# Norms, additions and slots of the last block: work moved from the vector engine to the scalar engine and GpSimd

## The reference

```python
x = x + _L1_ffn_ref(_layernorm(x), w_gate, w_up, w_down)      # first feed-forward
x = x + _L1_attn_b_ref(_layernorm(x), W_act, W_val, W_rec)    # a scan over time
x = x + _L1_ffn_ref(_layernorm(x), w_gate, w_up, w_down)      # second feed-forward, same weights

# _L1_ffn_ref
h = silu(x @ w_gate) * (x @ w_up)                              # 1024 wide
h_sparse = of every four neighbours of h the two of largest magnitude are kept
return h_sparse @ w_down

# _L1_attn_b_ref
ct = concatenate([x shifted by one position, x])
z = sigmoid(relu(ct @ W_act.T)); re, im = z in pairs
m = cummax(sqrt(re * re + im * im)); re, im = re / m, im / m
kv = associative_scan(complex product, (re, im))
return (kv @ W_val.T) * sigmoid(relu(ct @ W_rec.T)) ** 4
```

## Time and profile before

| what | us |
|---|---|
| median of three runs (1669.57 to 1683.92) | 1672.8 |
| the profiled execution | 1681.59 |
| its span | 1679.8 |
| this block, from its first instruction on DVE to the end | 1209.8 to 1679.8 |
| PE busy in the program (84% of the span) | 1409.5 |
| DVE busy (64%) | 1075.5 |
| ACT busy (37%) | 617.2 |
| POOL busy (17%) | 285.7 |

### The profile page before, as it was taken

The page is one execution under the profiler, slowest core; times in us unless marked ns, Lnnn a source line. Parts: engine busy times, 40 slices in busy tenths (PEclk is TensorE's granted clock), DMA queues, the critical chain, the costliest instruction groups (busy, mean ns, idle before and its releaser), DMA issues. The chain is left out here.

```text
span 1679.8 us, 21713 instructions
## 1 busy us (share of the span) xinstructions
PE 1409.5 (84%) x8144; PEld 1004.7 (60%) x8144; DVE 1075.5 (64%) x2163; ACT 617.2 (37%) x1144; POOL 285.7 (17%) x239
## 2 busy tenths in 40 slices
PE   2799999867999877799966899988579977979698
PEld 2455555456888756688864334433258765766576
DVE  5555454176877456778837566566267688787875
ACT  1254544333333222333321565656522422333221
POOL 1210000034433201233331330200120101011000
PEclk9799897678999988899986999999989998989899
DMA  8715320040000000000024421300000000000000
GB/s 179 97 31 67 53 26 1 1 146 1 1 1 1 1 0 1 1 1 1 1 59 51 86 54 33 48 2 1 1 1 1 1 0 1 1 1 0 13 13 25
DMA packets 23064, 42.01 MB, mean 25 GB/s; under 512 B 4705, under 2 KB 6497, under 8 KB 22833
## 3 DMA queue, kind: packets, MB, share of 16 engines
q1 hardware_dynamic: 22960, 40.64, 13.2%
HBM read 14.54 MB, written 2.10 MB: 10 GB/s over the span
## 5 line engine op out<-in xcount | busy, mean ns | idle before, releaser
L1285 DVE TENSOR_REDUCE attn_negm<-ps 128x2 f32<-128x1024 f32 (+3 forms) x256 | 256.1, 1021 | 124.1 <-PE ps L923 66.3
L1133 ACT ACTIVATE attn_probs<-ps 128x512 f32<-128x512 f32 (+3 forms) x512 | 237.0, 515 | 200.6 <-PE ps L946 124.4
L453 POOL TENSOR_TENSOR moe_h_low<-moe_h,moe_h_high 128x512 fp32r<-128x512 f32 x96 | 137.0, 1429 | 331.7 <-ACT moe_h_high L403 331.7
L937 PE MATMUL ps<-attn_qs,attn_ks 64*128 64x512 f32 (+3 forms) x512 | 156.9, 426 | 37.9 <-ACT attn_probs L1133 35.6
L1645 PE MATMUL ps<-sb_f_down,tail_h 128*128 128x256 f32 x512 | 129.8, 401 | 56.8 <-DVE x L1915 41.1
L1645 PEld LDWEIGHTS ps<-sb_f_down,tail_h 128*128 128x128 f32 x512 | 101.2, 200 | 78.1 <-DVE x L1915 44.1
L913 PE MATMUL ps<-attn_ks,attn_qs 63*128 63x512 f32 (+3 forms) x512 | 122.0, 473 | 29.3 <-DMA attn_ks<-attn_part_low 24.3
L420 ACT ACTIVATE moe_silu<-ps 128x512 f32<-128x512 f32 x96 | 57.4, 598 | 228.6 <-PE ps L326 228.5
L937 PEld LDWEIGHTS ps<-attn_qs,attn_ks 64*128 64x128 f32 x512 | 73.8, 198 | 102.2 <-ACT attn_probs L1133 96.7
L961 PE MATMUL ps<-attn_probs,attn_va 128*32 128x512 f32 (+3 forms) x1024 | 128.9, 580 | 0.0
L913 PEld LDWEIGHTS ps<-attn_ks,attn_qs 63*128 63x128 f32 x512 | 52.8, 202 | 97.8 <-issue 67.0
(11 more groups left out here) (317 smaller groups left out, 3282.8 us busy)
## 6 DMA issues: line engine op xcount, KB each, us to landing
attn_qs<-attn_part_high SPq DMA_DIRECT2D x64, 128.0 KB, 5.1
attn_qs<-attn_part_low SPq DMA_DIRECT2D x32, 128.0 KB, 4.7
attn_ks<-attn_part_high SPq DMA_DIRECT2D x32, 128.0 KB, 6.4
attn_ks<-attn_part_low SPq DMA_DIRECT2D x16, 128.0 KB, 7.1
out_x<-x SPq DMA_DIRECT2D x4, 512.0 KB, 2.6
x<-in_x SPq DMA_DIRECT2D x1, 1536.0 KB, 11.1
attn_qs<-attn_mT SPq DMA_DIRECT2D x64, 4.0 KB
moe_raw<-in_f_gate SPq DMA_DIRECT2D x2, 512.0 KB, 6.9
```

Source lines behind the costliest of these rows:

```text
L453: pool.tensor_tensor(hc.low[:, j % RING, :], h[:, j % RING, :], hc.high[:, j % RING, :], ALU.subtract).then_inc(low_done, 1)
L937: last = pe.matmul(ps[:, SC + k, 0:width2(kt)], ks[e:e + ROWS2, b % 2, key_tile(hd), kt * P:(kt + 1) * P], qs[e:e + ROWS2, b % 2, hd // 2, ...
L1133: act.activation(pr[:, s2 % RING, j, 0:n], ps[:, SC + k, 0:n], ACT.Exp, scale=HD ** -0.5).then_inc(exp_done, 1)
L1285: dve.tensor_reduce(m, ps[:, 2 * half:2 * half + 2, 0:width1(qt)], AX, ALU.max, negate=True).then_inc(r1_free, 1)
```

## The change

The eight norms of the scan's input and of its output leave DVE: ACT copies each row with its sum accumulated, POOL makes the negative mean of it, ACT squares (x - mean) with its sum accumulated, and POOL adds epsilon and raises to the power -0.5 (tensor_tensor with `ALU.pow`; the norms of sequences 1 to 3 at the start take their means and variances from DVE still, and this power from POOL). ACT copies the down sums out of PSUM into `dsum`, on which PE's next pass now waits (`sum_done`), and DVE adds `dsum` to x in one instruction of 128x1024 ahead of the slot's product. The inverse and the scan's output are put ahead of DVE's product too. The array of the scan lies with its segments outermost in a row (`zz`, [P, 2, S1, NS]), so that levels and trees read neighbours in memory; the fill writes into a second array `zt` in order of time, to which ACT copies what the fill doesn't write (`totals`). The running maximum is taken before the root. Jobs stand in other slots. POOL forms the low halves of the weights only after the first norm.

```diff
+    for p in range(PASSES):
+        act_at[added(p) - 1].append(("sum", p))
+        dve_first[added(p)].append(("add", p))
     for b in range(B):
         s = scan_from(b)
-        dve_at[s].append(("stats", "s", b))
+        act_at[s].append(("moments", "s", b))
         pool_at[s].append(("normalise", "s", b))
-        pe_at[s + 2] += [("row", "s", b, c) for c in range(DC)]
-        act_at[s + 2] += [("row", "s", b, c) for c in range(DC)]
-        pe_at[s + 3].append(("act", b, 0))
-        pe_at[s + 4].append(("act", b, 1))
-        act_at[s + 3].append(("act", b, 0))
-        act_at[s + 4] += [("act", b, 1), ("square", b)]
-        dve_at[s + 5].append(("sum", b))
-        act_at[s + 6].append(("root", b))
...
-        dve_at[s + 7] += [("divide", b)] + [("level", b, i) for i in (1, 2, 3)]
-        dve_at[s + 8] += [("level", b, i) for i in (4, 5, 6, 7)]
-        dve_at[s + 9] += [("tree", b, d) for d in TREE[:3]]
-        dve_at[s + 10] += [("tree", b, d) for d in TREE[3:]]
-        dve_at[s + 11].append(("fill", b))
-        pe_at[s + 6].append(("rec", b, 0))
-        act_at[s + 6].append(("rec", b, 0))
-        pe_at[s + 8].append(("rec", b, 1))
-        act_at[s + 8].append(("rec", b, 1))
-        pe_at[s + 12] += [("out", b, m) for m in range(2)]
-        dve_at[s + 12] += [("out", b, m) for m in range(2)]
-        dve_at[s + 13].append(("stats", "f", B + b))
+        pe_at[s + 1] += [("row", "s", b, c) for c in range(DC)]
+        act_at[s + 1] += [("row", "s", b, c) for c in range(DC)]
+        pe_at[s + 2] += [("act", b, 0), ("act", b, 1)]
+        act_at[s + 2] += [("act", b, 0), ("act", b, 1), ("square", b)]
+        dve_at[s + 3] += [("sum", b), ("peak", b)]
+        act_at[s + 3].append(("root", b))
+        dve_first[s + 4].append(("invert", b))
+        dve_at[s + 4] += [("divide", b), ("level", b, 1)]
+        pe_at[s + 5].append(("rec", b, 0))
+        act_at[s + 5].append(("rec", b, 0))
+        dve_at[s + 5].append(("level", b, 2))
+        pe_at[s + 6].append(("rec", b, 1))
+        act_at[s + 6].append(("rec", b, 1))
+        dve_at[s + 6].append(("level", b, 3))
+        dve_at[s + 7] += [("level", b, i) for i in (4, 5, 6)]
+        dve_at[s + 8] += [("level", b, 7)] + [("tree", b, d) for d in TREE[:2]]
+        dve_at[s + 9] += [("tree", b, d) for d in TREE[2:5]]
+        dve_at[s + 10] += [("tree", b, d) for d in TREE[5:]] + [("fill", b)]
+        act_at[s + 10].append(("totals", b))
+        pe_at[s + 11] += [("out", b, m) for m in range(2)]
+        dve_first[s + 13].append(("out", b))
+        act_at[s + 13].append(("moments", "f", B + b))
         pool_at[s + 13].append(("normalise", "f", B + b))
         pe_at[s + 15] += [("row", "f", B + b, c) for c in range(DC)]
         act_at[s + 15] += [("row", "f", B + b, c) for c in range(DC)]
         dve_at[s + 15] += [("row", "f", B + b, c) for c in range(DC)]
 
+    NORMS = [job[1:] for at in act_at for job in at if job[0] == "moments"]
     jobs = Turns([6, 7])
     early = [("row", "f", 0, c) for c in range(DC)]
     for todo in [early, *pe_at]:
...
             def value(b, m):
                 bank = take_bank(("out", b, m))
                 pe.wait_ge(filled, b + 1)
+                pe.wait_ge(totals_done, b + 1)
                 for i in range(2):
...
                 p, j = m // FC, m % FC
                 if j == 0:
-                    at_least(pe, x_done, p)
+                    at_least(pe, sum_done, p)
                 pe.wait_ge(sel_done, m // QUAD + 1)
                 for t in range(NT):
...
+            def root(b):
+                act.wait_ge(peak_ready, b + 1)
+                act.activation(sq[:, 1, :], sq[:, 1, :], ACT.Sqrt).then_inc(root_ready, 1)
+
+            def down_sum(p):
+                act.wait_ge(down_done, FC * (p + 1))
+                at_least(act, x_done, p)
+                act.activation(dsum[:, :, :], ps[:, DOWN:DOWN + 2, :], ACT.Copy).then_inc(sum_done, 1)
+
+            def moments(kind, k):
+                b = k % B
+                n, turn = nb[kind], NORMS.index((kind, k)) + 1
+                at_least(act, squared, turn - 1)
+                if kind == "s":
+                    act.wait_ge(x_done, b + 1)
+                else:
+                    act.wait_ge(x_scanned, b + 1)
+                if b > 0:
+                    act.wait_ge(xn_ready[kind], k)
+                for t in range(NT):
+                    last = act.activation(seen[:, t, :], x[:, NT * b + t, :], ACT.Copy, accum_out=n.sums[:, t:t + 1])
+                last.then_inc(summed, 1)
+                act.wait_ge(means_ready, turn)
+                for t in range(NT):
+                    last = act.activation(seen[:, t, :], x[:, NT * b + t, :], ACT.Square, bias=n.minus[:, t:t + 1],
+                                          accum_out=n.var[:, t:t + 1])
+                last.then_inc(squared, 1)
+
+            def totals(b):
+                if b > 0:
+                    act.wait_ge(ready, jobs.number[("out", b - 1, 1)])
+                act.wait_ge(scan_steps, 4 * (S1 - 1 + len(TREE) + 1) * b + 4 * (S1 - 1 + len(TREE)))
+                act.activation(segments[:, :, S1 - 1, :], zz[:, :, S1 - 1, :], ACT.Copy)
+                act.activation(segments[:, :, 0:S1 - 1, 0], zz[:, :, 0:S1 - 1, 0], ACT.Copy).then_inc(totals_done, 1)
...
+            cn = Chain(pool, root_steps, 1)
+
+            def means_and_roots(kind, b):
+                n, turn = nb[kind], NORMS.index((kind, b if kind == "s" else B + b)) + 1
+                pool.wait_ge(summed, turn)
+                pool.tensor_scalar(n.minus[:, :], n.sums[:, :], -1.0 / D, None, ALU.mult).then_inc(means_ready, 1)
+                pool.wait_ge(squared, turn)
+                pool.wait_ge(means_ready, turn)
+                cn.step(pool.tensor_scalar(n.var[:, :], n.var[:, :], 1.0 / D, EPS, ALU.mult, ALU.add))
+
             def normalise(kind, k):
                 if kind == "f" and k < B:
-                    pool.wait_ge(rest_ready, 1)
-                    m, y, c0, row0 = minus_rest, nb_rest.y, NT * (k - 1), NT * k
+                    pool.wait_ge(rest_ready, 2)
+                    n, c0, row0 = nb_rest, NT * (k - 1), NT * k
                 else:
                     b = k % B
-                    pool.wait_ge(stats_ready[kind], b + 1)
-                    m, y, c0, row0 = minus[kind], nb[kind].y, 0, NT * b
+                    means_and_roots(kind, b)
+                    n, c0, row0 = nb[kind], 0, NT * b
...
                     pool.wait_ge(ready, jobs.number[before])
                 for t in range(NT):
-                    last = pool.tensor_scalar(xn[kind][:, t, :], x[:, row0 + t, :], m[:, c0 + t:c0 + t + 1], y[:, c0 + t:c0 + t + 1],
+                    last = pool.tensor_scalar(xn[kind][:, t, :], x[:, row0 + t, :], n.minus[:, c0 + t:c0 + t + 1], n.y[:, c0 + t:c0 + t + 1],
                                               ALU.add, ALU.mult)
                 last.then_inc(xn_ready[kind], 1)
 
+            pool.memset(power[:, :], -0.5).then_inc(root_steps, 1)
+            cn.start(0)
+            cn.n = 1
+            cn.sync()
+
+            pool.wait_ge(xn_ready["f"], 1)
             for k, (n, at) in enumerate(parts):
                 pool.wait_ge(w_high, k + 1)
...
             def sum_of_squares(b):
                 dve.wait_ge(sq_ready, b + 1)
                 dve.tensor_tensor(sq[:, 0, :], sq[:, 0, :], sq[:, 1, :], ALU.add).then_inc(sum_ready, 1)
 
             def peak(b):
-
-                cp.start(b)
-                dve.wait_ge(mag_ready, b + 1)
-                cp.step(dve.tensor_tensor_scan(sq[:, 0, :], sq[:, 1, :], sq[:, 1, :], 0.0, ALU.max, ALU.max))
-                cp.step(dve.reciprocal(sq[:, 1, :], sq[:, 0, :]))
-                cp.end()
+                dve.wait_ge(sum_ready, b + 1)
+                dve.tensor_tensor_scan(sq[:, 1, :], sq[:, 0, :], sq[:, 0, :], 0.0, ALU.max, ALU.max).then_inc(peak_ready, 1)
+
+            def invert(b):
+                dve.wait_ge(root_ready, b + 1)
+                dve.reciprocal(sq[:, 0, :], sq[:, 1, :]).then_inc(inverted, 1)
 
             def divide(b):
-                if b > 0:
-                    dve.wait_ge(ready, jobs.number[("out", b - 1, 1)])
-                dve.scalar_tensor_tensor(zz[:, :, :], z[:, :, :], 1.0, sq[:, 1, :].unsqueeze(1).broadcast_to([P, 2, T]),
-                                         ALU.add, ALU.mult).then_inc(divided, 1)
+                at_least(dve, totals_done, b)
+                dve.wait_ge(inverted, b + 1)
+                inverse = sq[:, 0, :].rearrange("p (n s) -> p s n", s=S1)
+                for k in range(2):
+                    last = dve.scalar_tensor_tensor(zz[:, k, :, :], z[:, k, :].rearrange("p (n s) -> p s n", s=S1), 1.0, inverse,
+                                                    ALU.add, ALU.mult)
+                last.then_inc(divided, 1)
                 cx.start(b)
                 dve.wait_ge(divided, b + 1)
 
...
@@ -1822,47 +1913,50 @@
```

(29 more changed lines are left out.)

130 lines of the change are left out of this document (73 added, 57 removed).

## The result

| kernel | median, us | runs | lowest to highest |
|---|---|---|---|
| before | 1683.4 | 15 | 1669.6 to 1687.8 |
| after | 1666.8 | 15 | 1658.8 to 1675.4 |

The ratio is 0.9921, 95% interval 0.9893 to 0.9949: 0.8% less, some 13 us, where I forecast 19.8 us or 1.2%. Of the 13.8 us between forecast and median, 10.6 are the base: the three runs of before that the prediction knew had their median at 1672.8, the fifteen at 1683.4. The rest, 3.2, is the gain itself: 16.6 between the medians.

A forecast was written before the change was run, and what follows sets the result against it. The prediction took the order of hand-offs within a pass as the bound, DVE's load its largest part. Terms -6, +12.6, -15, -13 and +1.6 gave -19.8, from 1672.8 to 1653 us; range 1633 to 1671.

The forecast's parts named there:

- a chain of 63.7: Pass with a scan: successive steps on ACT, POOL, PE and DVE sum to 63.7 us; with hand-offs and lower clock 66.3.
- The wait for the down sums: PE's 11.06 us wait until DVE adds the down sums to x; it goes, with ACT's 1.06 copy hidden.
- the first item of the chain: Scan norm from sums to scaling on ACT and POOL: 9.8 us; PE waits some 6, lower clock costs 1.1.
- Pass 1: Pass 1 of the block: whole scan chain within eight slots, 54.4 to 67 us, +12.6.
- The start: Block's start to the first addition: first norm ready sooner, chunk 0 about 6 us sooner, net -6.
- pass 5: Pass 5: DVE's work until the fill 19 us, output products 3.7; 45 where 58.2 stood, -13.
- the end: Passes 6 and 7 unchanged; behind the last down product copy 1.06 and addition 1.22 replace a 0.69 half, +1.6.
- The three signs of error: Power several us; PE's wait for rows gone; ACT's wait for means making DVE stand for silu over 25.8 us.
- the loss by the power: Rival: POOL's power on the path to the rows makes the kernel slower, 1683 us at 8 us; chance 0.10.
- The slower chain: Rival: scalings at 5.27 and full 2 us of lower clock, pass 69 us, time 1664; chance 0.22.
- The shorter chain: Rival: cheaper power, means, scalings and levels, no lower clock, pass 62.7 us, time 1639; chance 0.20.
- DVE's load alone: Rival: gain from 10.8 us less on DVE in three passes, pass 1 not losing, 1635 us; no own chance.

The follow-up runs named there:

- x1: The changed kernel with only the slot table put back to that of the kernel before: 1642.95 us, ratio 0.9784 to before.
- x4: The changed kernel with a slot table chosen for the shortest walk, rows at s + 2: 1631.55 us, ratio 0.9743 to before.
- w1: The changed kernel with 38 overwritten PE matmuls put ahead of the scan norm's rows: 1657.3 us, ratio 0.9865 to before.
- z1: The changed kernel with POOL's power computed four times in the scan's norms: 1674.8 us, ratio 0.9986 to before.
- w2: The changed kernel with sequence 3's row transposes for pass 3 in slot 19, not 20: 1658.6 us, ratio 0.9876 to before.
- z3: x1 with the norms of the scan's input and output on DVE, as before: 1657.6 us, ratio 0.9864 to before.
- x3: The changed kernel with the scan norm's four scalings on DVE instead of POOL: 1646.1 us, ratio 0.9813 to before.
- z4: x4 with the scan norm's scalings on DVE, as in x3: 1630.3 us, ratio 0.9697 to before.

## Why the prediction was right in kind and wrong in size

**The order of hand-offs is the bound: right, and more narrowly than I said.** In every variant a pass is PE's busy time plus PE's idle time, and the first hardly moves between these four: 57.4 before, 57.8 after, 57.9 in x1, 57.5 in x4. What differs is the idle part: 14.0, 10.1, 7.3 and 3.7. I had put the pass down to a chain of 63.7 through all four engines. The trace of after shows only its first piece: from the addition to the rows PE has 2.52 us of work, the end of a chunk; from the rows on it is never short of work (55.25 of 55.45). My later items (reciprocal, levels, silu, selection) bound nothing there. I had called 57.4 PE's floor, but that figure holds products at the lower clock, 2 us of them behind the wait of the earlier trace rows.

**The wait for the down sums goes: right.** No such wait is left; the copy takes 1.02 on ACT and is hidden but for the last pass's (forecast 1.06). What is late next is the norm, as forecast, but PE's wait is 9.9, not 6.

**The step that failed is the first item of the chain**, "sums, mean, squares, variance, power, scaling: 5.4 + 1.1 + 3.3 = 9.8", with its lower clock of 1.1. From the addition's end to the scaled rows it is 11.1 (1420.36 to 1431.43). The parts: ACT's sums and squares 4.1 (0.40 and 0.50 with a reading that overlaps), 1.3 less than forecast; the power 1.04, 0.5 more; the scalings 5.35, 2.05 more. The lower clock behind the wait costs 2.5 (w1), 1.4 more. Together 2.7 a pass; the pass came out 1.5 above the forecast. The rest of the chain failed too, but as a path and with little error in the sum: I had 53.9 and 1.5 of hand-offs for it, and from the rows to the next addition the pass takes 56.8, of which 2.5 are the lower clock, so 54.3. That is PE's own work and no chain through four engines, and that the two sums lie 1.1 apart is luck.

I had written against the scalings at 5.27 that "the walk puts the trees there". The walk took POOL's and DVE's start for independent. They are tied: the norm on ACT holds back both the scaling and the silu behind which the comparisons stand. By the Trainium skill (SBUF — State Buffer, Who interferes with whom) a VectorE instruction with two SBUF inputs contends with a GpSimd one that reads SBUF, and the lock is exclusive. The trace agrees in kind: 2.16 alone, 5.35 with 3.49 of comparisons beside it. But the first scaling stands through three comparisons in a row, where I had let each scaling wait for one short step. And z1 shows that most of the standing goes to whichever instructions of POOL meet the comparisons: there the powers do, and the scalings take 2.39.

**Pass 1: right in kind, 5.2 short.** "The scan now runs through the whole chain within eight slots" gave 67. The missing item was a bank: rows of another sequence, behind comparisons, ahead of the first rec product, worth 10.1 (w2). Without it the pass takes 62.1, so my other items there were 5 too high. My walk did not carry the banks' owners into that slot.

**The start, pass 5, and the end** came within 1.6 of their terms, in part by luck. PE's chunk 0 began at 1213.62, 10.7 after the block's start where it was 16.8, so 6.1 sooner as forecast. In pass 5 (46.8 against 45) DVE reached the end of the fill 17.9 after its addition ended, where I had 19, although the fill's outputs took 0.96 each, with the step of eight numbers in writing, against 0.61 before; I had priced that step only for reading. What I missed is the clock. PE waits 7.87 for the fill, and the output products that I had at 3.7 take 6.61, at a granted clock of 0.55:

```profile
1574.40 6.61 PE L1651 MATMUL ps<-sb_s_val,tail_zt 128*128 128x256 f32 x16 [7.87 <-DVEq L1934]
```

At the end +1.6 came out as +1.6 from other terms. Copy and addition end 2.3 behind the last down product where the additions ended 1.3 behind it, 1.0 more; both halves had waited for that product before, and I had charged one. The last 32 down products took 8.85 at a granted clock of 0.81, where before they took 7.17 at 1.00, and pass 6 took 1.0 less.

**The three signs of error.** The power is 1.04, so the loss by the power did not come; z1 shows what 3.1 more would have cost: 6 in the block, 11 by the ratios. My rule of four times the excess would have given 12.4; the part that runs beside the comparisons costs less, so 5 us above my price would have taken less than the 20 that I gave for it. PE's wait for the rows is there. DVE's wait for silu did grow, from 25.8 to 43.1, but not by POOL's means, for which ACT waits 4.4 in all eight norms. The longest (8.8, in pass 1) ends with this silu, which stands behind ACT's jobs for the two act products:

```profile
1303.12 0.60 ACT L1726 ACTIVATE tail_z<-ps 128x512 f32<-128x512 f32 x1 [5.96 <-PE ps L1631]
1306.55 0.60 ACT L1726 ACTIVATE tail_z<-ps 128x512 f32<-128x512 f32 x1 [2.84 <-PE ps L1631]
1307.18 1.06 ACT L1732 ACTIVATE tail_z<-tail_z 128x1024 f32<-128x1024 f32 x1
1308.27 1.15 ACT L1733 ACTIVATE tail_sq<-tail_z,tail_halfone 128x1024 f32<-128x1024 f32 x1
1309.33 0.58 ACT L1819 ACTIVATE tail_silu<-ps 128x512 f32<-128x512 f32 x1
```

**The rivals.** The slower chain (scalings 5.27, full price of the clock, 1664, chance 0.22) is what happened in its mechanism: 5.35 and 2.5. Its pass of 69 was 1.2 too long. That its 1664 lies near the measured 1666.8 is luck: it stands on the same base of 1672.8 and gives a gain of 8.8. I gave it less than half of my own case's chance, for a walk whose start times I had not held against each other. The shorter chain is not this kernel's; x4 reached 61.2, but with scalings of 5.69 that PE had work to cover. The rival "DVE's load alone" had no chance of its own; z3 against x1 gives the load 11.9 us of the block once the slots allow it. Two sums of that part don't come out. From -14 to +19 around 1653 is 1639 to 1672, not 1633 to 1671. And 1635 for DVE's load alone has no term for pass 5, whose 13 were in the forecast.

**What I never asked** was whether the slots themselves are good. I took them as given and priced the pass that they make. The block by parts, each with the one before it: copied down sums 470.0 to 464.4; inverse, division, layout, additions ahead and the start (10.2 of it before the first addition), still in the slots of before, 450.1; the norms moved, 438.2; the change's slots, **459.9**; slots chosen for the waits, 426.5. The operations are worth 31.8 us, and the new slots gave back 21.7 of them; w2 shows that a single job makes 10.1 of the 15.0 that pass 1 lost. A row of the trace before could have raised the question: pass 1 took 54.4 with a scan beside it, and I forecast its loss of 12.6 without asking what it buys. It bought nothing: passes 2 to 4 were shorter in the old slots as well.

## What to carry to other kernels

When a wait goes, list PE's (or the fullest engine's) idle stretches of a pass and ask of each how much work stands ahead of the awaited step; in this kernel slots that cover the waits gave 33.4 us (x4) and a faster scaling 19.2 (x3), and with those slots the faster scaling gave nothing (z4). Where one engine releases two others at the same moment, look what the two do to each other before pricing either alone. And price a reordering apart from the operations that come with it: here the operations gained 31.8 us and the order lost 21.7.

## What the runs showed of the hardware

- POOL's power (tensor_tensor) on 128x4 took 1.04 us, while a tensor_scalar on the same 128x4 took 0.19 to 0.23 in the norms of the scan's input (in those of its output, up to 1.07 for one of them). With DVE's comparisons beside them four powers took 5.79.
- Four scalings of 128x256 on POOL: 2.16 alone, 5.35 when the comparisons start 0.33 before them, of which the first scaling has 3.42; on DVE 1.38.
- ACT's sums over 256 numbers took 0.40 (copy) and 0.50 (square with a bias), and the reading of the accumulator 0.19, of which some 0.1 overlaps: 0.40 and 0.49 from one to the next.
- After a wait of 9.92 us PE ran at a granted clock of 0.50 and 0.59 (6.19 us in all). 2.2 to 2.8 us of a pass are lost by it, and 38 products whose results are overwritten bring them back (w1). After waits of 11.70 and 11.71 in z1 the same stretch had 0.73 and 0.77.
- DVE with a step of eight numbers in the output, 441 elements: 0.96 instead of 0.61; with neighbours in the inputs, 128 elements: 0.31 and 0.29 instead of 0.39.
